# Attention block with routed experts: weights in five chunks, tile owners on GpSimd, and values ahead of the first QKV tile

## What is computed

```python
xn = layernorm(x)
q, k, v = split(xn @ wqkv.T)                  # 16 heads of 64
q, k = rope(rmsnorm(q, q_norm_w)), rope(rmsnorm(k, k_norm_w))
attn = softmax(causal(q @ k.T / 8))
out = (attn @ v) @ wo.T
chosen = argmax(xn @ gate_w.T)                # one of 8 experts for each row
ffn = xn + xn @ expert_w[chosen].T
return x + out + ffn
```

## Time and profile before

| what | value |
|---|---|
| median of 3 runs | 1976.66 us (1975.61 to 1977.33) |
| profiled execution, its own time | 1976.26 us |
| its span, first to last instruction | 1974.3 us |
| mean granted TensorE clock | 0.995 of full speed |
| busy: TensorE, VectorE, ScalarE, GpSimd | 1925.1, 1719.8, 1608.1, 1384.6 us |

### The profile page before, as it was taken

One profiled execution on the slowest core, in us unless ns is written; L12 is line 12 of the kernel. 1 busy time (PEld: TensorE's weight loads), 2 busy tenths in 40 slices (PEclk: granted clock), 3 DMA queues, 4 the chain that ended last, 5 costly groups with the idle time before them and its releaser, 6 DMA issues.

```text
span 1974.3 us, 51278 instructions
## 1 busy us (share of the span) xinstructions
PE 1925.1 (98%) x17288; PEld 1678.8 (85%) x17288; DVE 1719.8 (87%) x3936; ACT 1608.1 (81%) x5095; POOL 1384.6 (70%) x2023
## 2 busy tenths in 40 slices
PE   5999999999999999999999999999999999999996
PEld 5888888888888888888888888888888888888885
DVE  6988888898898888888988888888889888898875
ACT  4888888888888888888888888888888888888774
POOL 7877766677756877667775687766777578766753
PEclk8999999999999999999999999999999999999998
DMA  6110211212211132111331122212222112221344
GB/s 209 60 55 20 71 60 52 63 47 79 92 65 50 46 95 92 53 46 55 97 96 51 60 71 75 78 49 66 71 70 86 56 55 71 69 88 50 102 142 145
DMA packets 84561, 145.98 MB, mean 74 GB/s; under 512 B 9808, under 2 KB 63184, under 8 KB 84176
## 3 DMA queue, kind: packets, MB, share of 16 engines
q1 hardware_dynamic: 78160, 125.93, 19.8%
q0 software_dynamic: 6144, 16.79, 2.7%
HBM read 102.05 MB, written 40.63 MB: 72 GB/s over the span
## 4 chain that ended last, share of the span: by engine, by line
PE 91%; DVE 5%; issue 2%; POOL 1%; ACT 1%; DMA 1%; DVEq 0%; POOLq 0%
PE ps_g L814 41%; PE ps_g L936 14%; PE ps_g L947 13%; PE ps_s L895 10%; PE ps_g L876 6%; PE ps_g L895 2%; PE ps_s L890 2%; DVE neg_max L1130 2%; PE ps_g L890 1%; PE ps_g L841 1%; DVE prob L1142 1%; PE ps_g L823 1%; DVE ln_stat L1015 0%; POOL xn L578 0%; ACT prob L680 0%
## 5 line engine op out<-in xcount | busy, mean ns | idle before, releaser
L548 POOL TENSOR_TENSOR qk_rot<-qk_cos,qk_sin 128x128 f32<-128x128 f32 x1024 | 443.2, 464 | 482.0 <-PE ps_g L876 426.2
L814 PE MATMUL ps_g<-w_qkv,xn_t 128*128 128x384 f32 (+1 forms) x3072 | 636.2, 350 | 7.8 <-DVE w_qkv L1240 4.8
L814 PEld LDWEIGHTS ps_g<-w_qkv,xn_t 128*128 128x128 f32 x3072 | 523.2, 190 | 31.8 <-issue 22.6
L554 POOL TENSOR_TENSOR rms_inv<-ss,neg_half 128x8 f32<-128x8 f32 x256 | 425.2, 1661 | 0.0
L680 ACT ACTIVATE prob<-ps_s,neg_max 128x512 f32<-128x512 f32 (+2 forms) x768 | 417.5, 567 | 0.1
L688 ACT ACTIVATE prob_t<-ps_g 128x512 f32<-128x512 f32 (+2 forms) x768 | 394.1, 535 | 14.9 <-PE ps_g L936 13.3
L936 PE MATMUL ps_g<-ident,prob 128*128 128x128 f32 x2560 | 367.2, 274 | 13.6 <-DVE prob L1142 5.3
L559 POOL TENSOR_TENSOR qk_rot<-qk_rot,rms_inv 128x256 f32<-128x256 f32 x512 | 319.1, 644 | 20.1
L936 PEld LDWEIGHTS ps_g<-ident,prob 128*128 128x128 f32 x2560 | 300.6, 141 | 29.9 <-DVE prob L1142 14.5
L947 PE MATMUL ps_g<-prob_t,v 128*64 128x512 f32 (+3 forms) x2048 | 305.6, 441 | 3.2 <-ACT prob_t L688 2.3
L1130 DVE TENSOR_REDUCE neg_max<-ps_s 128x2 f32<-128x1024 f32 (+2 forms) x384 | 308.5, 860 | 0.0
(11 more groups left out here) (118 smaller groups left out, 3044.3 us busy)
## 6 DMA issues: line engine op xcount, KB each, us to landing
w_tile<-w_dram SPq DMA_DIRECT2D x120, 512.0 KB, 3.4
x_rows_s<-x_dram SPq DMA_DIRECT2D x120, 128.0 KB, 2.0
y_dram<-y_rows_s SPq DMA_DIRECT2D x120, 128.0 KB, 1.7
xin<-in_x SPq DMA_DIRECT2D x16, 512.0 KB, 4.1
out<-acc SPq DMA_DIRECT2D x15, 512.0 KB, 2.9
w_dram<-w_tile SPq DMA_DIRECT2D x8, 512.0 KB, 2.9
x_dram<-xn SPq DMA_DIRECT2D x2, 1920.0 KB, 18.9
y_back<-in_expert_t SPq DMA_DIRECT2D x8, 256.0 KB, 4.1
```

Of the source, the lines that this page charges most:

```text
L548: r = pool.tensor_tensor(rot[:, :, a, :], cos[:, :, a, :], sin[:, :, 1 - a, :], ALU.add)
L554: pool.tensor_tensor(rms_inv[:, ts[0]:ts[-1] + 1, :], ss[:, ts[0]:ts[-1] + 1, :], neg_half[:, :, :], ALU.pow).then_inc(s_pool_self, 1)
L814: r = pe.matmul(ps, lhs(a, c), rhs(b, c), start=(c == parts[0] and (a, b) == TERMS[0]), stop=(c == parts[-1] and (a, b) == TERMS[-1]))
```

## The change

Four things are changed.

- **Values first.** `values(u - 1)` now stands ahead of `qkv(u + 2, 0)` in every unit, on TensorE, and the copies of their results are exchanged likewise on ScalarE and VectorE (`take_o` ahead of `take_qkv` and `rope_products`) and in `uses`.
- **Weights.** Ten chunks in place of six (`STAGES`): pair 0, pair 1 (384 columns), pairs 2 and 3, pairs 4 and 5, pairs 6 and 7 (768 columns each), two halves of each. The chunks of pair 1 are split ahead of the loop, those of pairs 2 and 3 in turn -1, and the last four one by one in the turns 0 to 3, on ScalarE ahead of `softmax(u, 0)` and on VectorE behind `row_max`. They go to other staging places, and the expert weights are loaded ahead of the zeros for the scattered rows.
- **Owners.** VectorE's `find_tiles` is cut in two: `find_passed` (two instructions, in the unit of `find_slots`) stays on VectorE, and `find_tiles` on GpSimd adds the counts up with five small instructions.
- **Last rows.** The last group's rows are scattered in three units (3, 3 and 2 tiles of rows) in place of two (4 and 4), and the rows of the group before it come back one unit earlier.

```diff
@@ back_in, added_in
-                if u == (U + half if g == G - 1 else g * GROUP * PAIRS + (29 if g < G - 2 else 28) + 3 * half):
+                if u == (U + half if g == G - 1 else g * GROUP * PAIRS + (29 if g < G - 2 else 27) + 3 * half):
...
-                last = U + 1 + half if g == G - 1 else min(U, g * GROUP * PAIRS + (31 if g < G - 2 else 30) + 3 * half)
+                last = U + 1 + half if g == G - 1 else min(U, g * GROUP * PAIRS + (31 if g < G - 2 else 29) + 3 * half)
@@ uses
-                found += ["qkv0"] * live(u + 2) + ["o"] * live(u - 1)
+                found += ["o"] * live(u - 1) + ["qkv0"] * live(u + 2)
@@ scatters
-            for n in range(2):
+            for n in range(3):
                 g = slots_in(u - n)
                 if g == G - 1:
-                    return g, range(NT * n, NT * n + NT)
+                    return g, range(3 * n, min(3 * n + 3, GT))
@@ weight_chunks
+        STAGES = (0, 1, 2, 4, 6, PAIRS)
...
-            stop = (0, E + 3 * PW, E + PAIRS * 3 * PW // 2, E + PAIRS * 3 * PW)
+            stop = [E * (p > 0) + p * 3 * PW for p in STAGES]
@@ gpsimd
+            def find_tiles(g):
...
+                pool.wait_ge(s_passed, g + 1)
+                for n in (4, 2, 1):
+                    own(pool.tensor_tensor(passed[:, :, 0:n], passed[:, :, 0:n], passed[:, :, n:2 * n], ALU.add))
+                own(pool.tensor_scalar(tile_expert[:, :], passed[:, :, 0], float(E - 1), None, ALU.min))
+                pool.tensor_copy(tile_expert_i[:, g % 2, :], tile_expert[:, :]).then_inc(s_tiles, 1)
@@ gpsimd unit
+                found = ranks_in(u - 3) if u >= U - PAIRS else ranks_in(u - 2)
+                if found is not None:
+                    find_tiles(found)
@@ scalar unit
+                if 0 <= u < 4:
+                    high_weights(6 + u)
...
-                if u == -1:
-                    high_weights(2)
-                    high_weights(3)
-                if live(u + 2) and not turns_x(u):
-                    take_qkv(u + 2, 0)
                 if live(u - 1):
                     take_o(u - 1)
-                if turns_x(u):
+                if live(u + 2):
                     take_qkv(u + 2, 0)
@@ tensor
-                if u in (1, PAIRS // 2) and t == 0:
-                    pe.wait_ge(s_w_free, 4 if u == 1 else 6)
+                if u in STAGES[1:-1] and t == 0:
+                    pe.wait_ge(s_w_free, 2 * STAGES.index(u) + 2)
...
                 if turns_x(u):
                     transpose_xn(batch_of(u) + 1)
-                elif live(u + 2):
-                    qkv(u + 2, 0)
                 if live(u - 1):
                     values(u - 1)
-                if turns_x(u):
+                if live(u + 2):
                     qkv(u + 2, 0)
@@ vector unit
-                if u == -1:
-                    low_weights(2)
-                    low_weights(3)
+                if 0 <= u < 4:
+                    low_weights(6 + u)
...
+                    find_passed(slots_in(u))
...
-                if slots_in(u - 1) is not None and slots_in(u - 1) < G - 1:
-                    find_tiles(slots_in(u - 1))
```

More of the change, by code:

```diff
@@ L160, in block_program @@
         s_masks_pe = sem("s_masks_pe")
-        w_loaded = [sem(f"w_loaded{i}") for i in range(6)]
+        w_loaded = [sem(f"w_loaded{i}") for i in range(10)]
         s_w_free = sem("s_w_free")
@@ L410, in loads @@
             return 16 * (i // of + 1)
+        STAGES = (0, 1, 2, 4, 6, PAIRS)
         staged = (prob_t[:, :, :, :].rearrange("p a t n -> p (a t n)"), prob[:, :, :].rearrange("p h n -> p (h n)"),
-                  acc[:, 0:2, :, :].rearrange("p a t c -> p (a t c)"))
+                  acc[:, 1, :, :].rearrange("p t c -> p (t c)"), x_rows_s[:, :, :].rearrange("p i c -> p (i c)"),
+                  xn[:, 1, 1:, :].rearrange("p t c -> p (t c)"))
         def weight_chunks():
-            stop = (0, E + 3 * PW, E + PAIRS * 3 * PW // 2, E + PAIRS * 3 * PW)
-            places = ((0, 0), (0, stop[1]), (0, 2 * stop[1]), (0, stop[1] + stop[2]), (1, 0), (2, 0))
+            stop = [E * (p > 0) + p * 3 * PW for p in STAGES]
+            one, two = stop[1], 3 * PW
+            places = ((0, 0), (0, one), (0, 2 * one), (0, 2 * one + two), (1, 0), (1, 2 * two),
+                      (2, 0), (3, 0), (4, 0), (2, 0))
             for n, (to, at) in enumerate(places):
@@ L429, in _, with load_weights @@
             sp.dma_start(xin[:, :, :], x_rows[0]).then_inc(s_x_first, 16)
[L430 to L434, removed]
+            def load_weights(chunks):
+                for n in chunks:
+                    dst, src, raw = tuple(weight_chunks())[n]
+                    sp.dma_start(raw, src).then_inc(w_loaded[n], 16)
+            load_weights(range(0, 2))
+            for dst, table in ((nw[:, :, :], norm_w), (t_cos[:, :, 0, :], rope_cos), (t_sin[:, :, 0, :], rope_sin)):
+                sp.dma_start(dst, table).then_inc(s_consts_pool, 16)
+            load_weights(range(2, 6))
             sp.dma_start(wo_raw, wo_t).then_inc(s_wo_loaded, 16)
+            for e in range(2):
+                sp.dma_start(we_raw[:, e, :, :], expert_t[:, :, e, :]).then_inc(s_we_loaded[e], 16)
+            load_weights(range(6, 9))
             sp.wait_ge(s_x_zero, 1)
@@ L467, in unit @@
             def unit(u):
+                if u == 1:
+                    sp.wait_ge(s_w_free, 7)
+                    load_weights(range(9, 10))
                 if 0 <= u < E:
@@ L587, in split_weights, with own @@
                                    ALU.subtract).then_inc(s_we_split, 1)
+            def find_tiles(g):
+                def own(r):
+                    r.then_inc(s_pool_self, 1)
+                    pool.wait_ge(s_pool_self, seen(s_pool_self))
+                pool.wait_ge(s_passed, g + 1)
[3 more added lines that the diff above has]
+                pool.tensor_copy(tile_expert_i[:, g % 2, :], tile_expert[:, :]).then_inc(s_tiles, 1)
             def start_rows(b, half):
@@ L595, in start_rows @@
                     pool.wait_ge(s_xn_pe, b + 1)
-                if b < 4 and half == 0:
-                    pool.wait_ge(s_w_free, 6)
+                if b == 1 and half == 0:
+                    pool.wait_ge(s_w_free, 10)
                 pool.tensor_tensor(acc[:, b % 4, rows, :], xin[:, rows, :], xn[:, b % GROUP, rows, :], ALU.add)\
@@ L795, in _ @@
             take_xt(0)
+            high_weights(2)
+            high_weights(3)
             for u in units:
@@ L1080, in find_slots, with find_passed @@
                 dve.tensor_copy(slot_i[:, g % 2, :], slot[:, :]).then_inc(s_slots, 1)
-            def find_tiles(g):
+            def find_passed(g):
                 own(dve.tensor_tensor(end_tile[:, :], first_tile[:, :], tiles_of_e[:, :], ALU.add))
-                own(dve.tensor_tensor(passed[:, :, :], tile_no[:, :].unsqueeze(2).to_broadcast([P, NS, E]),
-                                      end_tile[:, :].unsqueeze(1).to_broadcast([P, NS, E]), ALU.is_ge))
-                own(dve.tensor_reduce(tile_expert[:, :], passed[:, :, :], AX.X, ALU.add))
-                own(dve.tensor_scalar(tile_expert[:, :], tile_expert[:, :], float(E - 1), None, ALU.min))
-                dve.tensor_copy(tile_expert_i[:, g % 2, :], tile_expert[:, :]).then_inc(s_tiles, 1)
+                dve.tensor_tensor(passed[:, :, :], tile_no[:, :].unsqueeze(2).to_broadcast([P, NS, E]),
+                                  end_tile[:, :].unsqueeze(1).to_broadcast([P, NS, E]), ALU.is_ge).then_inc(s_passed, 1)
             def take_xs(u, i):
@@ L1208, in unit @@
                     take_xs(u, i)
-                if live(u + 2) and not turns_x(u):
-                    rope_products(u + 2, 0)
                 if live(u - 1):
                     take_o(u - 1)
-                if turns_x(u):
+                if live(u + 2):
                     rope_products(u + 2, 0)
```

10 lines of the change are left out of this document (7 added, 3 removed).

## The result

| | us |
|---|---|
| before, median | 1976.61 (1975.61 to 1977.33) |
| changed, median | 2027.27 (2026.98 to 2027.42) |
| ratio | 1.0256, 95% interval 1.0239 to 1.0274 |
| changed, profiled execution: own time, span, mean granted clock | 2027.13, 2025.3, 0.997 |

The changed kernel is 2.6% slower: 50.7 us by the medians and 51.0 by the spans of the profiled executions (2025.3 - 1974.3), where the sum gave 58.3. The forecast of 2035 was 8 us too high, and the time lies within its range.

The account below looks back on a forecast made before the run. TensorE bounds the kernel (91% of the chain). Terms: 71.9 + 0.3 - 8.0 - 1.7 - 3.2 + 1.5 - 2.5 = +58.3 us, giving about 2035 against 1976.66, 3.0% slower; range 2019 to 2050, 8 in 10.

Parts of the forecast that it names:

- weights: start, chunks in units 1 to 3: Start gains 3.2 us; smaller weight chunks ahead of ScalarE's softmax in units 1 to 3 lose 1.5.
- owners: Transposes behind the second QKV tile: find_tiles leaving VectorE ends the x_cols_s delays, 8.0 us gained (5 to 9).
- last rows: k_t wait, end: Unit 121's wait for k_t goes, 1.7 us gained; two gathers fewer before the last addition, 2.5 gained.
- values first: Values wait for ScalarE's copied probabilities: 71.9 us lost in 106 units, 0.3 together in units 122 to 125.
- Steady units: 88 units with an expert product: 0.76 lost at the values, stretch behind 4.52 for 4.68, 0.60 lost each.
- not slower: Rival: TensorE passes the waiting values and does the first QKV tile meanwhile; 1962 us, 4 in 100.
- nothing given back, or new waits behind: Rival: the run of twelve QKV products gains nothing, 2054 us, or later transposes wait too, to 2070; 11 in 100.
- Half hidden: Rival: ScalarE reaches the copy for the values sooner, 0.3 lost a unit, 1994 us; 6 in 100.
- Other units: 18 units without an expert product ahead of the values, read from unit 9: 1.06 us lost each.
- Start: GpSimd's q and k scaling for unit 0 gains 2.2 us, VectorE's splits about 1: 3.2 together (1 to 4.8).

Follow-up runs that it names:

- the last rows undone: Kernel before with weights and owners as changed, order of values and QKV and last rows as before: 1967.88 us, ratio 0.9957.
- the longer copy: Changed kernel with ScalarE's copy of the last transposed probabilities written as two instructions of half the size: 2034.45 us, ratio 1.0291.
- transposes earlier: Changed kernel with the last two transposes of the probabilities put inside the scores and ScalarE's copy of them ahead of the softmax: 1995.56 us, ratio 1.0097.
- owners undone: Changed kernel, values still first, with find_tiles whole on VectorE again: 2029.75 us, ratio 1.0266.

## Why the prediction was right, and where its sizes were off

The terms, measured by the spans of one profiled execution each, as the parts are added one behind the other. The runs of the kernels with the weights alone and with the last rows undone spread over 2.7 and 3.0, so the first three rows are no better than a microsecond or two:

| part | forecast | measured | spans |
|---|---|---|---|
| weights: start, chunks in units 1 to 3 | -3.2 + 1.5 = -1.7 | -2.4 | 1974.3 to 1971.9 |
| owners | -8.0 | -7.1 | to 1964.8 |
| last rows: k_t wait, end | -1.7 - 2.5 = -4.2 | -4.6 | to 1960.2 |
| values first | 71.9 + 0.3 = 72.2 | +65.1 | to 2025.3 |
| sum | +58.3 | +51.0 | |

**Steady units: right.** Rows 4 to 6 gave 0.76 lost at the values, a stretch of 4.52 behind them and 0.60 a unit. The changed unit 66 shows 0.76, 4.52 and 15.39 in place of 14.79. TensorE passes nothing ahead of the waiting values: the twelve QKV products start 2.30 behind them, as in unit 6. The rule on program order (the Trainium skill, TensorE: Matmul & The Clock Gate, section The mechanism) agrees with that; the rival *not slower*, in which TensorE does the QKV tile meanwhile, is out. The rival *nothing given back, or new waits behind* is out as well, since the run of twelve gives its 0.16 and no later wait appears. *Half hidden* is out by the copy's place, unchanged at 1.28 behind the start of the softmax.

**Other units: the term mis-sized.** The 71.9 counted two kinds of units. Measured against the kernel with the order undone, the 61 units with nothing else in them lose 0.61 each. The 18 that were put at 1.06 don't all lose it. Unit 9 of the changed kernel (compare) has the row that was expected:

```profile
170.76 2.38 PE L975 MATMUL ps_g<-prob_t,v 128*64 128x512 f32 x16 [1.14 <-ACT prob_t L717]
173.06 2.39 PE L842 MATMUL ps_g<-w_qkv,xn_t 128*128 128x384 f32 x12
175.29 0.60 PE L964 MATMUL ps_g<-ident,prob 128*128 128x128 f32 x4
```

The wait of 1.14 is the 1.38 of the forecast, less the overlap with the transposes ahead of it, as 0.51 is that of 0.76; and 4.53 follows. But of the 12 early units only five lose 1.06 to 1.09. Five others (1, 3, 7, 9, 13) lose 0.36 to 0.59; they are 14.4 to 14.9 long with the old order already, where the first five are 13.9 to 14.0. Two (8 and 11) lose 0.95 and 0.85. Together that is 9.7, where 12.7 was counted. The six later ones lose 0.58 each, in all 3.5 for 6.4; of the units with an expert tile some (28, 44, ...) lose 0.82 and some (31, 47, ...) 0.38. With the new order most of these units come out at one length, whatever they took before: 15.03 to 15.05 in units 4, 5 and 8 to 13, which took 13.95 to 14.56 with the old order, and 15.39 in units 28 and 31, which took 14.57 and 15.02. So the chain to the values sets the length there (the longer copy makes each of the 18 longer by 0.04 to 0.08 as well), and what a unit loses is that length less its old one. That the old length was set by other work is argued from these lengths; I didn't test it by itself. I had taken unit 9 for all 18 and unit 66 for the 88 without looking at what else lies in them. That is nearly the whole of the miss: 72.2 - 65.1 = 7.1 of 7.3. That the other three terms add so little is luck in part: they are off by -0.7, +0.9 and -0.4, which nearly cancel.

**Find_tiles: right in size, wrong as a sum.** With the old order the owners gain 6.3 to 7.1, near the 8.0, and the wait for x_cols_s at the transposes is all but gone (0.7 once, for 4.1 in seven units). With the new order they gain 2.5. I said "TensorE now comes there 0.6 later" and took the whole 8.0 as gained; the two can't both be counted, since a TensorE that comes later has lost the 0.6 already. By order of adding, the overlap is booked under the owners or under the values; the sum of the table holds only in the order in which it stands.

**Start: the place was right, the way not.** The wait for the weights goes, and GpSimd's scaling comes late next, as forecast; it takes 1.18 without VectorE's wide split beside it, as forecast. TensorE transposes q and k at 27.20, not at 29.40: 2.2 earlier, the forecast's own number. But the scores of unit 0 start at the same time as before, 32.96. The rows of TensorE in the changed kernel, and below them stretches of its trace (length; busy time and instructions of TensorE, of its weight loads, VectorE, ScalarE and GpSimd; granted clock; DMA share; GB/s):

```profile
27.20 1.97 PE L904 MATMUL ps_g<-ident,qk_rot 128*128 128x128 f32 x8 [5.08 <-POOL qk_rot L573]
28.82 3.80 PE L842 MATMUL ps_g<-w_qkv,xn_t 128*128 128x384 f32 x12
...
39.99 1.53 PE L964 MATMUL ps_g<-ident,prob 128*128 128x128 f32 x12 [2.59 <-DVE prob L1167]
```

```profile
27.20:30.00 2.80, 2.80 (x12) 2.80 (x13) 0.85 (x2) 1.39 (x3) 0.75 (x2) 0.50 0.15 51
30.00:32.50 2.50, 2.50 (x10) 2.30 (x8) 2.46 (x3) 1.71 (x4) 2.50 (x4) 0.60 0.00 0
32.50:36.00 3.50, 3.50 (x52) 3.35 (x52) 3.50 (x9) 2.84 (x8) 3.42 (x7) 1.00 0.03 5
...
40.00:46.40 6.40, 5.98 (x56) 5.29 (x56) 5.78 (x15) 5.38 (x17) 6.39 (x8) 1.00 0.56 166
```

The granted clock behind the wait of 5.08 is 0.50, the lower level (1.2 GHz), 0.60 on average in the next stretch, and 1.00, the upper level (2.4 GHz), from 32.5 on. The transposes take 1.97 and twelve QKV products 3.80. Before, TensorE stood idle too (4.84), but ahead of an earlier run of QKV products, which took 3.85; the transposes and the products behind ran at the upper level then, in 1.10 and 2.36:

```profile
29.40 1.10 PE L876 MATMUL ps_g<-ident,qk_rot 128*128 128x128 f32 x8 [1.14 <-POOL qk_rot L559]
30.25 2.36 PE L814 MATMUL ps_g<-w_qkv,xn_t 128*128 128x384 f32 x12
```

The slow stretch has moved behind GpSimd's scaling, and gives back 2.3, all of the gain. In unit 0 it goes the other way. TensorE waits 2.59 there and not 4.41, the clock behind it is 1.00, and the twelve transposes take 1.53. Before, in the same place, TensorE's rows and the stretch of the trace were:

```profile
42.88 2.82 PE L936 MATMUL ps_g<-ident,prob 128*128 128x128 f32 x12 [4.41 <-DVE prob L1142]
45.50 1.92 PE L876 MATMUL ps_g<-ident,qk_rot 128*128 128x128 f32 x8
47.06 2.85 PE L814 MATMUL ps_g<-w_qkv,xn_t 128*128 128x384 f32 x12
```

```profile
42.90:50.90 8.00, 8.00 (x54) 7.76 (x56) 5.80 (x16) 6.39 (x19) 6.52 (x9) 0.67 0.30 99
```

Unit 0 is 4.5 shorter (46.38 - 32.96 from scores to scores, for 50.91 - 32.96): 2.9 from the earlier start of those transposes, 1.6 from the clock, net of two small new waits. So the start gains 4.5, not 3.2 (its upper bound was 4.8), and the 2.2 that was read from GpSimd's scaling is no part of it.

How the 4.5 divides is that of one execution. Seven of the kernels above have the same chunks. Their unit 0 starts its scores between 31.62 and 33.11, and their unit 1 between 46.20 and 47.11, where it is 50.91 before: 3.8 to 4.7 gained. In the kernel with the weights alone, the transposes of q and k and the QKV products behind them took 5.0, not 5.8, and its scores start 1.3 earlier than before; but its wait in unit 0 was longer, and the transposes behind it ran at a lower clock:

```profile
39.41 2.27 PE L951 MATMUL ps_g<-ident,prob 128*128 128x128 f32 x12 [3.35 <-DVE prob L1157]
```

From 39.41 to 43.40 the granted clock is 0.58 there. It fell likewise behind the waits of 3.07 (transposes earlier) and 3.27 (owners undone) in that place, and stayed at 1.00 in the other kernels, whose waits were 2.36 to 2.95. That the clock falls when TensorE stands idle and comes back up once it works is what the Trainium skill says (TensorE: Matmul & The Clock Gate, section What's actually happening), and the trace agrees with it: 0.50 behind the 5.08, 1.00 behind the 2.59.

**End and last rows: right.** The k_t wait of unit 121 is gone. In the changed kernel the eight gathers run from 2008.18 to 2017.03 and the last addition starts at 2021.24, 13.06 behind the first gather, where it was 15.65: 2.6 for the forecast's 2.5.

## What to carry to other kernels

Work of TensorE between a transpose and the product that needs its copied result is cover: taking it away costs start to start what the copy still lacks (0.76 here, in rows that could be read beforehand, of which 0.16 came back), in each unit that nothing else lengthens already, and shortening the copy's own queue gives little back. Look for a place where the new order already stands (unit 6) and read the price from its rows, then go through every kind of unit before multiplying. Gains that shorten a wait and a loss that makes another engine late overlap; the version to keep here is the change without its new order, 1962.17 us, 0.7% faster than before.

## What was not expected of the hardware

- At the start of the changed kernel, transposes that began 2.2 earlier gained nothing: they came right behind an idle time of 5.08, at a granted clock of 0.50, and with the QKV products behind them took 5.8 in place of 3.5. In unit 0 a wait that fell from 4.41 to 2.59 gained 1.6 beyond the earlier start.
- Two full-array transposes put into the middle of the scores, which run in pairs on 64 rows each, cost 0.35 a unit beyond their own 0.22, with no wait noted in the profile. The weight loads behind the cut started with their products, not 0.10 ahead of them; whether that is all of the 0.35 was not measured by itself and stays open.
- Two copies of 128x128 on ScalarE take 0.44 together, one of 128x256 takes 0.38. Each half takes 0.27 to 0.28, and the second starts 0.16 behind the first.
